# SyncE's load queue held to two loads in flight, four in the opening

## The reference, cut to what matters

```python
# x (128, 128, 512), cond_8 (128, 8), weight (8, 512, 512), mask (512, 512), bias (512,), all fp32
masked_w = weight * mask[None, :, :]
w_bot = jnp.einsum('bg,got->bot', y, masked_w)        # y = cond_8: one 512x512 matrix for each batch
return x + jnp.einsum('bnt,bot->bno', x, w_bot) + bias
```

## Time and profile before

| | |
|---|---|
| median of three runs | 588.17 us (587.94 to 589.99) |
| the profiled execution's own time | 590.58 us |
| its span, first to last instruction | 588.8 us |
| PE busy | 577.1 us (98%) |
| granted TensorE clock | 1.00 |
| loads sent by SP | 279: 128 of x, 112 of xn, 16 of weights and masks in the fourth unit, 23 of them in the opening |
| read and written in DRAM | 113.8 MB and 33.6 MB |

### The profile page before, as it was taken

How to read it: one execution, slowest core, us unless ns; L and a number is a source line. 1 busy time by engine, 2 the same in 40 slices (tenths; PEclk the granted TensorE clock), 3 DMA queues, 4 the chain that set the end, 5 groups by cost and what they waited for, 6 DMA issues and landing times.

```text
span 588.8 us, 20669 instructions
## 1 busy us (share of the span) xinstructions
PE 577.1 (98%) x9148; PEld 542.0 (92%) x9148; DVE 328.7 (56%) x600; ACT 160.5 (27%) x334; POOL 38.4 (7%) x34
## 2 busy tenths in 40 slices
PE   7899999999999999999999999999999999999998
PEld 4799999889998999989899899998999989999887
DVE  5562557346673476645666356663566635665333
ACT  5340444014440144302343023430234203441000
POOL 3430000000000011123110000000000000000000
PEclk9999999999999999999999999999999999999999
DMA  9978546884668869899676875769676795759842
GB/s 320 407 298 287 179 147 216 288 332 154 220 216 306 282 199 326 264 351 411 244 269 223 313 267 164 258 187 349 201 216 212 226 339 185 243 172 313 273 159 89
DMA packets 59849, 148.71 MB, mean 253 GB/s; under 512 B 6624, under 2 KB 7520, under 8 KB 59760
## 3 DMA queue, kind: packets, MB, share of 16 engines
q1 hardware_dynamic: 40176, 113.00, 57.4%
q10 hardware_dynamic: 19584, 34.39, 15.4%
HBM read 113.81 MB, written 33.55 MB: 250 GB/s over the span
## 4 chain that ended last, share of the span: by engine, by line
PE 96%; DMA 1%; issue 1%; POOL 1%; SPq 1%; DVE 0%; DVEq 0%; POOLq 0%
PE ps L592 43%; PE ps L611 34%; PE ps L562 19%; DMA xs<-in_mask 1%; POOL wm L284 1%; SPq L307 0%; SPq L313 0%; PE ps L545 0%; DVE wbot L440 0%; DVE staged L476 0%; DVEq L474 0%; POOLq L282 0%
## 5 line engine op out<-in xcount | busy, mean ns | idle before, releaser
L592 PE MATMUL ps<-wbot,xs 128*128 128x256 f32 (+1 forms) x1400 | 253.7, 343 | 0.8 <-DVE wbot L440 0.8
L592 PEld LDWEIGHTS ps<-wbot,xs 128*128 128x128 f32 x1400 | 227.1, 191 | 25.4 <-issue 1.6
L363 ACT ACTIVATE wbot<-ps 128x512 f32<-128x512 f32 (+2 forms) x277 | 140.8, 567 | 343.0 <-PE ps L562 337.1
L611 PE MATMUL ps<-wbot,xs 32*128 32x256 f32 x3584 | 220.9, 376 | 0.1
L440 DVE COPY wbot<-ps 128x512 f32<-128x512 f32 (+2 forms) x274 | 164.6, 646 | 93.2 <-PE ps L562 89.6
L611 PEld LDWEIGHTS ps<-wbot,xs 32*128 32x128 f32 x3584 | 188.1, 185 | 2.6 <-issue 1.0
L562 PEld LDWEIGHTS ps<-y_sb,wm 32*128 32x128 f32 x4096 | 144.8, 186 | 11.4 <-issue 7.0
L562 PE MATMUL ps<-y_sb,wm 32*128 32x128 f32 x4096 | 147.9, 273 | 5.9 <-issue 4.3
L476 DVE TENSOR_TENSOR staged<-ps,staged 128x256 f32<-128x256 f32 (+2 forms) x121 | 63.9, 544 | 140.5 <-PE ps L592 127.2
L458 DVE TENSOR_TENSOR staged<-staged,bias_sb 128x512 f32<-128x512 f32 (+2 forms) x121 | 79.3, 661 | 0.0
L284 POOL TENSOR_TENSOR wm<-wm,mask_sb 128x512 f32<-128x512 f32 x16 | 21.3, 1354 | 243.4 <-DMA mask_sb<-in_mask 243.4
(11 more groups left out here) (6 smaller groups left out, 1.5 us busy)
## 6 DMA issues: line engine op xcount, KB each, us to landing
xs<-in_x SPq DMA_DIRECT2D x128, 512.0 KB, 5.4
out<-staged ACTq DMA_DIRECT2D x127, 256.0 KB, 5.1
staged<-in_xn SPq DMA_DIRECT2D x112, 256.0 KB, 3.9
wm<-in_w SPq DMA_DIRECT2D x12, 512.0 KB, 8.5
mask_sb<-in_mask SPq DMA_DIRECT2D x8, 512.0 KB, 7.5
wm<-in_w SPq DMA_DIRECT2D x8, 256.0 KB, 5.9
xs<-in_mask SPq DMA_DIRECT2D x4, 512.0 KB, 13.0
xs<-in_mask SPq DMA_DIRECT2D x7, 256.0 KB, 6.3
```

Of the source, the lines that this page charges most:

```text
L363: eng.activation(tile_place(b, j, first, end), tile_sums(b, j, first, end), ACT.Copy).then_inc(s_ev_a, 1)
L592: ins = eng.matmul(bank[:, at:at + width], group[:, h, k, :], sums_of(slice(0, P), u, g, h, c, end, k), start=(k == 0), stop=(k == KT - 1))
L611: ins = eng.matmul(ps[BANK_OF[i, None]][:, 0:WIDTH[i]], xs[rows, X_AT[u, g] % XRING, h, k, :], sums_of(rows, u, g, h, c, end, k), start=(n ...
```

## The change

`stand_in_line` is called before every load that SP sends. It keeps a list of the loads so far, each with its semaphore and the number of times that this semaphore has been used. If at least `most` loads are in the list, SP waits until the load that stands `most` places back has landed, and then the new load is sent. `most` is 4 for the weights and masks of the first half and for the first ten x loads, and 2 for all others. No load changes its size, its place in the order, its buffer or the waits it had. The loads and stores that ACT sends aren't touched.

```diff
--- before.py
+++ after.py
@@ -119,6 +119,7 @@
 AHEAD = {1, 3, 5, 7, 8, 10, 12, 14}
 OWN_X = OUT_TILES // UNITS
 X_LEAD = 4
+FIRST_LINE, LINE = 4, 2
 
 
 BANK_OF, TAKEN_FROM = {}, {}
@@ -300,16 +301,28 @@
 
         @block.sync
         def _(eng):
+            sent = []
+
+            def stand_in_line(most, landing, times):
+
+                if len(sent) >= most:
+                    before, landings = sent[-most]
+                    eng.wait_ge(before, 16 * landings)
+                sent.append((landing, times))
+
             def load_w(s, c, count):
 
                 if s:
                     eng.wait_ge(s_s1, ((WINDOWS * s - 1) * CS + c + count) * TILES)
+                stand_in_line(LINE if s else FIRST_LINE, s_w[c], s + 1)
                 eng.dma_start(wm[:, c:c + count, :], w[s, :, c:c + count, :]).then_inc(s_w[c], 16)
                 if s:
                     if c >= MASKN:
                         masked(eng, s, c - 1)
+                    stand_in_line(LINE, s_mask[c], s + 1)
                     eng.dma_start(mask_sb[:, 0:count, :], mask[s, :, c:c + count, :]).then_inc(s_mask[c], 16)
                 elif c:
+                    stand_in_line(FIRST_LINE, s_mask[c], 1)
                     eng.dma_start(first_mask[:, c:c + count, :], mask[s, :, c:c + count, :]).then_inc(s_mask[c], 16)
 
             def load_x(n):
@@ -319,11 +332,13 @@
                     masked(eng, 0, n * 2 - 4)
                     masked(eng, 0, n * 2 - 3)
                 u, g = X_ORDER[n]
+                stand_in_line(LINE if n >= XRING else FIRST_LINE, s_x[n % XRING], n // XRING + 1)
                 eng.dma_start(xs[:, n % XRING, :, :, :], x[u % WINDOWS * GROUPS + g]).then_inc(s_x[n % XRING], 16)
 
             def load_xn(m):
 
                 stored(eng, m - OUTB)
+                stand_in_line(LINE, s_xn[m % OUTB], len(range(m, OWN_X - 1, -OUTB)))
                 eng.dma_start(staged_of(m), xn[m]).then_inc(s_xn[m % OUTB], 16)
 
             for c in range(HALF):
```

## The result

The changed kernel takes 617.54 us (615.67 to 617.9, four runs), against 589.08 us for the kernel before on the same chip: a ratio of 1.0473, 95% interval 1.0433 to 1.0512. That is 28 us slower where 5 were forecast, outside the range of 587.9 to 602.5. The direction was right; the size is near rival 2's 622 us, though not by rival 2's mechanism, as will be seen.

A forecast was written before the change was run, and what follows sets the result against it. PE was taken as the bound (577.1 of 588.8 us busy), so loads could only cost: opening 0.3 plus fourth unit's stall 4.7 makes 5.0 us, 593.2 us against the median of 588.17; range 587.9 to 602.5.

The forecast's parts named there:

- rival 2: Queue too slow everywhere: above 4.43 us per pair every unit falls behind; 622 us at 4.7, 603 at 4.45; chance 0.11.
- the deadline of 280.3: Fourth unit: tile 57's xn costs nothing if landed by 280.3 us; forecast landing 285.0, so PE stops once for 4.7 us.
- stores land sooner: Fourth unit: shallow queue lands stores sooner than 7.1 us, ending xn waits on them earlier; counted as nothing.
- the length of a link: Fourth unit's chain: one 512 KB landing per link, 3.75 us outside the dense part, 4.25 inside, mean 3.9.
- the last two sends: End of the fourth unit's chain: tile 57's xn goes out 0.4 us after the 19th load and lands 3.8 us later.
- The start of the chain: Fourth unit: chain of 19 loads counted from the x sent at about 209.8 us.
- the next tight places: Fourth unit's last xn and the last weights: bear 4.05 us per link, more than the mean of 3.9; nothing added.
- +0.3: Opening, window of four: net loss taken as 0.3 us, between up to 0.7 us won and 1 us lost.
- Four in flight are just enough: Opening: fifth mask, SP's ninth load, sent at 8.1 and landing in 2.8 us, at 10.9 instead of 10.79.
- My upper bound: Opening: ten loads until the last 256 KB mask cost 0.1 us more each if four don't fill the queue, 1 us.
- The sign that I had named: Opening: first group's first piece starts within 1 us of 19.3; off by more than 1 us would show the forecast wrong.
- The stall's place: Fourth unit: PE stops once, around 280 us, behind tile 57's xn; late additions inside a dense part not felt at once.

The follow-up runs named there:

- e4: Changed kernel, window of two in the main loop for x and xn alone, fourth unit's weights and masks uncounted, none in the opening: 593.3 us, ratio 1.0072 to kernel before.
- e8: Changed kernel without opening window, main loop window of two, but three for SP's loads 101 to 182 (fourth unit): 589.1 us, ratio 1.0017 to kernel before.
- e5: Changed kernel without opening window, main loop window of two, ACT storing only 64 of each tile's 512 columns: 597.3 us, ratio 1.0162 to kernel before.
- e2: Changed kernel with only the main loop's window of two, none in the opening: 609.4 us, ratio 1.0325 to kernel before.
- e9: As e2, but fourth unit's weights and masks read from a DRAM copy with each 512 KB pair in one piece: 609.6 us, ratio 1.0319 to kernel before.
- e10: As e2, but only the first of the fourth unit's eight mask loads is made and used for all pairs: 593.6 us, ratio 1.0071 to kernel before.
- e1: Changed kernel with only the opening's window of four, none in the main loop: 594.4 us, ratio 1.0081 to kernel before.
- e7: Changed kernel with the window of four for SP's first fifteen loads (256 KB) alone, none after: 593.1 us, ratio 1.0081 to kernel before.
- e3: Changed kernel with a window of three in the main loop, none in the opening: 590.1 us, ratio 1.0021 to kernel before.

## Why the prediction was wrong

**Right.** After the opening PE had nothing to win; ordinary units are carried by two in flight, and the fourth is not (e4, e8); the loss comes as waits of DVE for xn loads near 280 us, and the deadline of 280.3 holds (the table above); stores land sooner (median 4.0 instead of 7.1 us) and it helps nothing, since SP hardly waits for them any more (12.6 us instead of 292.5, none of it in the fourth unit's chain). Nor was it rival 2: the other units lose 2 us at most each, although they are near their limit of 4.43 us. The median landing of an x is 4.5 us from 60 to 205 us and 3.9 from 350 to 500 us in the kernel after.

**The step that failed first: the length of a link.** "Outside the dense part 3.75, inside 4.25", 3.94 on average, was 4.44. Eighteen times 0.50 is 9 us. The eight samples of the earlier trace rows were sent at moments that the old order made quiet, most of them when a group of PE's was done and the last store had landed 1.5 us or more before, so that the next stores were only sent while they were under way. A chain that always sends meets the stores at any moment. e5 fits this: with the stores cut to an eighth the chain runs at 3.93 (that this is just the 3.94 that I had forecast with whole stores is chance). In the stretch of e2 there are 16 stores to 18 links; seven eighths of their transfer, at 0.66 us for a whole one (256 KB at 399 GB/s), make an estimate of 0.51 us per link, and 0.46 were measured. Nearly all of a store's transfer thus seems to end up in a link, although the DMA engines aren't full: the chain waits for each landing, and what comes between isn't made good. Why even e5 doesn't reach the quick link of 3.45 is in part the masks in the chain, 4.3 us on average against 3.7 for x; e9 excludes their spacing in DRAM, and why they are slow is open.

**How much that step explains.** The xn of tile 57 landed 24.9 us after 280.3 instead of 4.7. Of these 20 us the links make 8.9, the late start of the chain 8.7 (5.8 from the opening, 2.9 of its own), and the last two sends 2.5: the xn went out 2.1 us behind the mask and took 4.7, where I had 0.4 and 3.8. Another 1.7 us are lost behind it, which makes the 26.6 of the span.

**The start of the chain.** I let it begin with the x sent at 209.8, as if the lead were whole. In e2 this x goes out at 212.75, when the load two places before it has landed, not when PE is done with a group as in the kernel before: 3 us more. The lead had been used up in the units before, where PE doesn't feel it.

**Put at nothing: the next tight places.** At my mean link of 3.9 they cost nothing; at 4.39 they do. In e2 PE stands 3.1 us in three places between 319 and 335 us, twice for DVE's copies and once for POOL's product with the last mask, and 2.0 us in the kernel after.

**Left out: the clock.** After a stop of 11 us PE resumes at a granted clock of 0.50. The whole kernel spends 9.1 us more in the same matmuls, 5.8 in e2, and my sum had no such term. How much of it is a cost of its own isn't shown. In e2 and in the kernel after, the slow matmuls right behind the long stop fall before the landing of tile 57's xn, for which PE would have had to stop anyway, and the table leaves 0.6 to 1.1 us between the landing and the burst. In e10, where PE's stops are short, 1.9 and 1.6 us, it leaves 1.5 us.

**The opening: +0.3 was 4.8.** "Four in flight are just enough" took the empty queue's landing for the landing in a queue of four. In the kernel after the ninth load landed at 11.11, where I had said 10.9, but at 11.78 in e1 and 12.22 in e7, and from the twelfth on all three are about 2 us late: I followed one load, and the term was wrong by 4.5 us. The DMA engines went from 385 to 301 GB/s (e1), and this sum of bytes comes due later: PE's ninth burst was 3.6 us late in e1 and 3.2 in the kernel after. My upper bound, 0.1 us for each of ten loads, had this in it as 1 us. PE's mean clock from 10 to 20 us is 0.83 in e1 and 0.86 in the kernel after, but the clock isn't the cause: in e7 it stays at 1.00, and the ninth burst is 4.3 us late. The sign that I had named came: the first group's first piece started at 21.6 instead of 19.3 us.

**The stall's place.** I wrote that DVE's lateness isn't felt at once inside a dense part; true, but at its end all of it is, before tile 57 comes up. So PE stops earlier and for other tiles than I had said; how late it comes out of it is still set by tile 57's xn, as the table shows.

**The range.** It let in 4.25 per link throughout as its upper end, while the six samples in the dense part had a mean of 4.7. Its own rival priced 4.7 at 18 us for the fourth unit alone. Yet the link by itself wouldn't have left the range: at the measured 4.44 the forecast's arithmetic gives 13.6 us, with 0.3 for the opening 602.1 us, just under 602.5. What went beyond it are the terms at or near nothing, the opening, the late start of the chain, its last two sends and the tight places behind it.

## What to carry to other kernels

A window on a load queue turns it into a chain: its price is the number of links times a whole landing, by the mean and not by the median, and other transfers (the stores here) lengthen each landing. Compare that with the deadline of the thickest stretch, not with the mean rate; here one more load in flight (e3, e8) made 19 us disappear. When landings under a window are estimated from a trace without it, look at what released the samples: loads that were sent when others had just ended tell of a quiet machine. Ask also where the chain starts: a queue that is near its limit in the units before comes late to the thickest one. Where bytes are what limits, compare bytes moved in a stretch (385 against 300 GB/s), since a single landing hides how far the engines were ahead. And where PE will stand, look whether its slower matmuls afterwards are covered by the next wait before adding them.

## What the runs showed of the hardware that was not expected

Four loads of 256 KB in flight moved 297 to 301 GB/s, eight 388, the unbounded queue 385. In the fourth unit stores took a median of 7.1 us to land where loads were queued unbounded (209.7 to 268.6 us) and 4.0 with two in flight (213 to 297 us), without any edit of their own. During and after a stop of 11.24 us PE's granted clock was 0.50: so in the 5 us from 290 on, of which PE worked 3.27, and 0.78 on average in the 5 us after that.
